# Dequantization of units 11 to 41 by chains of Prelu, with GpSimd taking the first right pass and the high half, and the kernel's maximum through TensorE

## What is computed

```python
xn = _layernorm(x)                       # x: (4, 512, 512) f32, 2048 tokens of 512
K  = _s4_kernel(...)                     # 512 numbers from 64 complex states
y  = irfft(rfft(xn, 1024) * rfft(K, 1024))[..., :512] + D * xn     # causal convolution
Wg, Wu = dequant_nf4(gate), dequant_nf4(up)     # (1792, 512) each, 4-bit codes as int32
Wd     = dequant_nf4(down)                      # (512, 1792), one absmax for 64 codes
h  = silu(xn @ Wg.T) * (xn @ Wu.T)
out = x + y + h @ Wd.T
```

## Time and profile before

| what | value |
|---|---|
| median of 3 runs | 467.42 us (466.54 to 467.91) |
| the profiled execution | 466.52 us, of which the profile's span is 464.7 us |
| PE busy | 446.5 us, 96% of the span |
| DVE busy | 400.2 us, 86% |
| ACT busy | 284.9 us, 61% |
| GpSimd busy | 61.5 us, 13% |
| TensorE clock granted | 1.0 in every stretch |

### The profile page before, as it was taken

How to read it: one execution, slowest core, us unless ns; L and a number is a source line. 1 busy time by engine, 2 the same in 40 slices (tenths; PEclk the granted TensorE clock), 3 DMA queues, 4 the chain that set the end, 5 groups by cost and what they waited for, 6 DMA issues and landing times.

```text
span 464.7 us, 7186 instructions
## 1 busy us (share of the span) xinstructions
PE 446.5 (96%) x2595; PEld 253.9 (55%) x2595; DVE 400.2 (86%) x658; ACT 284.9 (61%) x480; POOL 61.5 (13%) x116
## 2 busy tenths in 40 slices
PE   0699999999999999999999999999999999999997
PEld 0554444444444444444444444466544688888886
DVE  4899689979798887988999888876799899999993
ACT  7966565587597965769777696794132543545340
POOL 0464499400000000000001000023100000000000
PEclk9999999999999999999999999999999999999999
DMA  8482545122425234112132225256570021101111
GB/s 273 86 284 80 114 88 147 47 70 67 159 69 181 95 132 158 59 56 86 51 95 71 91 41 158 78 183 209 169 292 0 1 92 47 44 3 47 47 47 45
DMA packets 31830, 47.20 MB, mean 102 GB/s; under 512 B 13044, under 2 KB 14132, under 8 KB 31284
## 3 DMA queue, kind: packets, MB, share of 16 engines
q1 hardware_dynamic: 30516, 42.56, 30.0%
q0 software_dynamic: 1280, 4.20, 2.8%
HBM read 35.93 MB, written 8.72 MB: 96 GB/s over the span
## 4 chain that ended last, share of the span: by engine, by line
PE 90%; DVE 3%; POOL 2%; ACT 2%; DMA 1%; issue 1%; SPq 0%; POOLq 0%
PE bank L1875 34%; PE bank L2006 21%; PE bank L2108 21%; PE bank L2059 8%; PE bank L2049 6%; DMA work<-in_q_up 1%; POOL h L718 1%; PE bank L1910 1%; ACT h L816 0%; DVE h L1174 0%; DVE h L1337 0%; PE bank L1965 0%; DVE bank L1281 0%; DVE work L1167 0%; DVE work L1163 0%
## 5 line engine op out<-in xcount | busy, mean ns | idle before, releaser
L1875 PE MATMUL bank<-xT,w 128*128 128x512 f16 (+1 forms) x732 | 164.9, 378 | 1.9 <-DVE w L1174 1.7
L1875 PEld LDWEIGHTS bank<-xT,w 128*128 128x128 f16 x732 | 71.9, 99 | 86.5 <-DVE w L1174 2.1
L816 ACT ACTIVATE work<-work 128x512 f32<-128x512 int32 x136 | 77.8, 623 | 5.0 <-DVE work L1146 2.5
L2108 PE MATMUL bank<-wd,work 128*128 128x256 f16 x504 | 56.2, 273 | 0.0
L2108 PEld LDWEIGHTS bank<-wd,work 128*128 128x128 f16 (+1 forms) x504 | 49.3, 98 | 6.0
L2006 PE MATMUL bank<-h 128*128 128x512 f16 x198 | 48.1, 379 | 0.0
L1106 ACT ACTIVATE work<-h 128x896 f16<-128x896 f32 x30 | 27.9, 942 | 27.8 <-DVE h L1783 18.3
L2108 PE MATMUL bank<-h,work 128*128 128x256 f16 x378 | 42.2, 273 | 0.0
L2108 PEld LDWEIGHTS bank<-h,work 128*128 128x128 f16 x378 | 37.0, 98 | 4.3
L900 ACT ACTIVATE work<-bank,sc 128x512 f32<-128x512 f32 x45 | 30.4, 678 | 13.2 <-PE bank L1875 12.9
L2059 PE MATMUL bank<-wd,h 128*128 128x512 f16 x168 | 36.4, 379 | 0.0
(11 more groups left out here) (183 smaller groups left out, 643.3 us busy)
## 6 DMA issues: line engine op xcount, KB each, us to landing
h<-in_x SPq DMA_DIRECT2D x8, 512.0 KB, 6.2
moved<-h SPq DMA_DIRECT2D x4, 1024.0 KB, 4.7
xT<-in_x POOLq DMA_DIRECT2D x16, 256.0 KB, 3.4
h<-moved SPq DMA_DIRECT2D x4, 1024.0 KB, 10.5
out<-xT SPq DMA_DIRECT2D x15, 256.0 KB, 2.1
work<-in_q_gate SPq DMA_DIRECT2D x14, 256.0 KB, 2.7
work<-in_q_up SPq DMA_DIRECT2D x14, 256.0 KB, 2.9
work<-in_am_gate SPq DMA_DIRECT2D x28, 128.0 KB, 3.0
```

The lines of the kernel that those rows point to most:

```text
L816: nc.scalar.activation(knee_of(u, k), qs[:, u % 2, :], KNEE, scale=scale, bias=bias, alpha=below).then_inc(knee_done, 1)
L1875: mm = nc.tensor.matmul(out_b, weights(k)[:, unit, wl, f, :], xT[:, TPC * c + first:TPC * c + last, xl, f, :], start=(i == 0), stop=(i == ...
L2108: mm = nc.tensor.matmul(out_b, part, w, start=(n == 0), stop=(n == 3 * KT - 1))
```

## The change

- **CHAINED** becomes `range(11, UNITS)`: the units 11 to 41 are made by chains, not only the last four. Rooms for the whole tile rotate over three (`whole_of`).
- **The right chain** loses its first Prelu on ACT. GpSimd makes it as `max(code, c) - c` from the codes (`first_pass`, `L818` of the changed kernel), and ACT goes on from its result: six passes in the order l0 r0 l1 r1 l2 r2, where r0 waits for `first_done`.
- **The high half** of the units 11 to 37 (POOL_HALVES) moves from ACT to GpSimd (`weight_hi` there, `L831`); DVE's low half waits for `phi_done`. DVE's items of such a unit u are now WHOLE(u), low half of u-1, SCALED(u).
- **GpSimd's list** in the windows is first pass of u+1, then high half of u, for u = 11..37. `turned_rows()` (the eight copies) is called inside this loop, after the high half of unit 28. First passes of units 39 and 40 stand ahead of the reloads of x, that of 41 behind the fourth.
- **The maximum** over partitions: PE transposes the column of row maxima (`kernel_max`) after product 1 of window 13, DVE reduces and makes the powers in slot 2, PE spreads two numbers to all partitions by a matmul with ones (`kernel_scale`) after product 6, DVE makes the scales in slot 4 and the Toeplitz tiles in slot 5 of window 13 (before: slot 1). `ones` gets a room of its own.

```diff
-CHAIN_ORDER = ("r0", "l0", "r1", "l1", "r2", "l2", "r3")
+CHAIN_ORDER = ("l0", "r0", "l1", "r1", "l2", "r2")
-CHAINED = range(UNITS - 4, UNITS)
+CHAINED = range(11, UNITS)
+POOL_HALVES = range(CHAINED[0], UNITS - 4)
...
+        def room_read(u):
+            return dq_after(u - 1, LEFT) if u == CHAINED[0] else dq_after(u - 2, WHOLE)
...
-                if u >= 2:
-                    sp.wait_ge(knee_done, PASSES_AT[u - 2] + (2 if u - 2 in CHAINED else KNEES))
+                if u - 2 in CHAINED:
+                    sp.wait_ge(first_done, u - 2 - CHAINED[0] + 1)
+                    sp.wait_ge(knee_done, PASSES_AT[u - 2] + 1)
...
-            pool.wait_ge(u_done, 4)
-            for c in range(2):
-                for a in range(4):
-                    ...
-            pool.wait_ge(t_done, 3)
-            pool.partition_all_reduce(kmax, krow, P, bass.bass_isa.ReduceOp.max).then_inc(kmax_done, 1)
+            def first_pass(u):
+                pool.wait_ge(q_ld[u % 2], 16 * (u // 2 + 1))
+                pool.wait_ge(dq_done, room_read(u))
+                pool.tensor_scalar(chain_room(u, "r"), qs[:, u % 2, :], RIGHT_FROM, RIGHT_FROM,
+                                   ALU.max, ALU.subtract).then_inc(first_done, 1)
+            def weight_hi(u):
+                pool.wait_ge(dq_done, dq_after(u, SCALED))
+                ...
+                pool.tensor_scalar(weight_of(u)[HI], whole_of(u), scale_of(u), None, ALU.mult).then_inc(phi_done, 1)
+            pool.wait_ge(v_done, V_STEPS)
+            first_pass(CHAINED[0])
+            for u in POOL_HALVES:
+                first_pass(u + 1)
+                weight_hi(u)
+                if u == made_before(NM - 3) - 1:
+                    turned_rows()
+            first_pass(UNITS - 3)
+            first_pass(UNITS - 2)
             for t in range(NT):
                 pool.wait_ge(conv_done, t + 1)
                 pool.dma_start(res[:, t, :], x_v[:, t, :]).then_inc(xr_ld[t], 16)
+                if t == 3:
+                    first_pass(UNITS - 1)
...
+                elif side == "r":
+                    act.wait_ge(first_done, u - CHAINED[0] + 1)
...
                     if u in CHAINED:
-                        i += 2
+                        i = (3, 2, 4)[i]
...
+                if k == NM - 1:
+                    kernel_max()
...
+                if k == NM - 1:
+                    kernel_scale()
```

More of the change, by code:

```diff
@@ L133 @@
 DVE_AT = counted(lambda u: 3 if u in CHAINED else 5)
+ACT_HALVES = [u for u in range(UNITS) if u not in POOL_HALVES]
 ACT_AT = counted(lambda u: 1 + (u not in CHAINED) + (PASSES_AT[u + 2] - PASSES_AT[u + 1] if u + 1 < UNITS else 0))
@@ L214, in ffn_conv_kernel @@
         sc = sb("sc", [P, 34], F32)
+        ones = sb("ones", [3, P], F32)
         V = sb("V", [P, 2, 8], F32)
@@ L663, in _ @@
         def _(pool):
-            pool.memset(one3, 1.0).then_inc(one_done, 1)
+            pool.memset(ones[:], 1.0).then_inc(one_done, 1)
             pool.memset(ident[:], 0.0).then_inc(one_done, 1)
@@ L785, in _, with turned_rows @@
                 chained(pool.tensor_copy(V_halves[rows, :, 8 * half:8 * half + 8], V[rows]))
-            pool.wait_ge(u_done, 4)
-            for c in range(2):
-                for a in range(4):
-                    if a == 0:
-                        row = turns[:, 0, c:c + 1].to_broadcast([P, 4])
-                    else:
-                        row = turns[:, a, c:c + 3 * a + 1:a]
-                    pool.tensor_copy(turned[:, c, a, :], row).then_inc(turn_done, 1)
-            pool.wait_ge(t_done, 3)
-            pool.partition_all_reduce(kmax, krow, P, bass.bass_isa.ReduceOp.max).then_inc(kmax_done, 1)
+            def turned_rows():
+                pool.wait_ge(u_done, 4)
+                for c in range(2):
+                    for a in range(4):
+                        if a == 0:
+                            row = turns[:, 0, c:c + 1].to_broadcast([P, 4])
+                        else:
+                            row = turns[:, a, c:c + 3 * a + 1:a]
+                        pool.tensor_copy(turned[:, c, a, :], row).then_inc(turn_done, 1)
+            def first_pass(u):
[5 more added lines that the diff above has]
+                pool.wait_ge(dq_done, dq_after(u, SCALED))
+                unit = SEQ[u]
+                if unit < GU:
+                    before = room_before(unit // 2)
+                    if unit % 2 and before in BLOCKED:
+                        pool.wait_ge(m_done, m_at(before, 4))
+                    else:
+                        pool.wait_ge((gate_done, up_done)[unit % 2], WHOLE_COUNT[LAST_USE[before]])
+                pool.tensor_scalar(weight_of(u)[HI], whole_of(u), scale_of(u), None, ALU.mult).then_inc(phi_done, 1)
[8 more added lines that the diff above has]
+            first_pass(UNITS - 2)
             for t in range(NT):
@@ L805, in _ @@
             act.wait_ge(one_done, 1)
-            nc.scalar.activation(sil[0:1, 0, 0:1], one3[0:1, 0:1], ACT.Silu)
+            nc.scalar.activation(sil[0:1, 0, 0:1], ones[0:1, 0:1], ACT.Silu)
             def make_knee(u, k):
@@ L857, in weight_hi, with gate_copy @@
                 nc.scalar.activation(weight_of(u)[HI], whole_of(u), ACT.Copy, scale=scale_of(u)).then_inc(whi_done, 1)
-                if unit < GU and unit % 2 == 0 and unit // 2 in BLOCKED:
-                    k = unit // 2
-                    if k == BLOCKED[0]:
-                        act.wait_ge(xlo_done, NT)
-                    else:
-                        act.wait_ge(xs_lo, 4)
-                        act.wait_ge(w_done, 4 * blocked(k))
-                    nc.scalar.activation(sums_room(k)[0], whole_of(u), ACT.Copy, scale=scale_of(u)).then_inc(g_done, 1)
+            def gate_copy(u):
+                if SEQ[u] >= GU or SEQ[u] % 2 or SEQ[u] // 2 not in BLOCKED:
+                    return
+                k = SEQ[u] // 2
+                act.wait_ge(dq_done, dq_after(u, SCALED))
+                if k == BLOCKED[0]:
+                    act.wait_ge(xlo_done, NT)
+                else:
+                    act.wait_ge(xs_lo, 4)
+                    act.wait_ge(w_done, 4 * blocked(k))
+                nc.scalar.activation(sums_room(k)[0], whole_of(u), ACT.Copy, scale=scale_of(u)).then_inc(g_done, 1)
             def items(first, last):
@@ L874, in items @@
                     if p == ACT_AT[u]:
[L875 removed]
+                        if u - 1 in ACT_HALVES:
+                            weight_hi(u - 1)
+                        gate_copy(u - 1)
                     elif i == 0:
@@ L1916, in _ @@
             pe.wait_ge(sc_done, 7)
-            nc.tensor.matmul(bank[0][:, P:P + 6], one3, dg3, start=True, stop=True).then_inc(mx_bc, 1)
+            nc.tensor.matmul(bank[0][:, P:P + 6], ones[:], dg3, start=True, stop=True).then_inc(mx_bc, 1)
             turn(2)
@@ L1967, in kernel_line, with kernel_max, kernel_scale @@
                 mm.then_inc(toe_mm, 1)
+            def kernel_max():
+                pe.wait_ge(t_done, 3)
+                nc.tensor.transpose(bank[7][0:1, 0:P], krow, ident[:]).then_inc(km_tp, 1)
+            def kernel_scale():
+                pe.wait_ge(sc_done, KMAX_MADE)
+                nc.tensor.matmul(bank[7][:, P:P + 2], ones[0:1, :], sc[0:1, 17:19], start=True, stop=True).then_inc(km_bc, 1)
             def blocked_product(k, i):
```

63 lines of the change are left out of this document (40 added, 23 removed).

## The result

The changed kernel takes 473.11 us (median of 4, 472.24 to 473.30) against 467.09 us for the kernel before: 1.0124 times as long, interval 1.0103 to 1.0144, so 6.0 us more. The profiled execution took 473.30 us with a span of 471.5 us. I had forecast 470.0 us within 467.6 to 472.6: the direction was right, the size not, and the result lies outside the range.

The account below looks back on a forecast made before the run. PE was taken as the bound, busy 96% of the span and without a gap from 48 us on. Window 11's 1.8, window 4's 0.4 and the maximum's 0.4 made 2.6 us on 467.42: 470.0 us, range 467.6 to 472.6.

Parts of the forecast that it names:

- It can shorten the time only in the first 48 us, which it leaves alone but for one memset: Whole kernel: from 48 us PE has no gap, so the change is worth at most nothing.
- My third rival: Start: PE's wait for the identity shrinks with the reduction gone, 1.5 us at most, 466.3 us; chance 0.04.
- Window 11, 1.8 us: Ahead of product 3: unit 30's first pass queues behind the eight copies, the join comes late, PE waits 1.8 us.
- Window 4, 0.4 us: Window 3 into 4: r0 of unit 11 delays chunk 3's silu and the last `block_lo`; PE loses 0.4 us.
- Slow passes: Rival, windows 11 and 4 and fifth reload: GpSimd passes at 2.2 us add 2.5 us, 472.5 us; chance 0.14.
- Steady windows at nothing: Steady windows: GpSimd keeps up; PE would wait in every window only if a pass took over 3.4 us.
- The maximum: Window 13: two instructions added to PE's gapless row, 0.45 us if neither waits, taken as 0.4.
- The convolution: First passes of units 39 to 41 delay reloads of x, mostly hidden: 0, at most 0.7 us.
- DVE's busy time: Sign over the whole kernel: DVE's busy time lower by about 32 us, about 27 units x 2 x 0.6.
- the median I used: Starting point of the forecast for the kernel before: 467.42 us, to which 2.6 us were added.

Follow-up runs that it names:

- the old maximum: Changed kernel with GpSimd's reduction for the maximum again, ahead of unit 33's high half, copies behind unit 30's first pass, chunk 3's silu ahead in window 3: 479.37 us.
- the forms: Changed kernel with seven forms of a 128x512 step on GpSimd, three times each, behind the last reload of x, results not needed: 477.19 us.

## Why the prediction was wrong

- **"It can shorten the time only in the first 48 us, which it leaves alone but for one memset"**: this step failed, and with it the forecast. The reduction stands at 283 us in the kernel before, but its removal also takes away a stop of 9 us at 1.2 us, and without it GpSimd's chain of small steps beside DVE took 9.5 us and not 7.65, in every kernel that was run. It cost 2.9 us in the profiled execution: 1.3 us of late tokens and 1.6 us of lower clock; with the reduction put back the kernel took 470.63 us. My third rival had seen the tie between the reduction and the wait for the identity, and drew the wrong sign from it: the identity came at 1.3 us, PE then waited for DVE (10.0 us), and nothing was gained.
- **Window 11, 1.8 us**: measured 1.9 as a wait and 2.0 as PE's delay, by the mechanism named, and the run that moves the copies shows it. Two terms were off and nearly cancel, which is luck: the copies took 1.04 us and not 2.07, and the pass 2.31 and not 0.76 to 1.46. Before, DVE had step behind step beside the copies; now it was idle for the first 0.3 us and then ran one step on a bank. That this is why they were short is not shown. The quarter turn's end (forecast 249.3; it came at 253.65, which less the shift of 4.2 us that this window had by then is 249.4) and the way from the pass to the join's end (5.0 us for 5.1 to 5.2) were right. ACT's idle time ahead of r0 was 4.1 us for some 3.
- **Window 4, 0.4 us**: right place and chain of causes, mis-sized: 1.2 as a wait and 1.3 as PE's delay. The pass took 1.94 us, and DVE's steps beside the pass of unit 12 lost 0.35 us (L1267 0.83 for 0.48). With 1.94 us for 0.76 to 1.46 in the sum of the prediction the silu is 1.3 us late, and 1.3 + 0.35 - 0.46 = 1.2; 0.14 us from the block's end to PE's start, which the sum left out, make it 1.3. The rival of slow passes had given 1.1.
- **Slow passes**, 0.14: their size came true (2.08 us on the mean), their effect in window 11 did not add up, because of the copies. I had put too little on it: no row showed this form, and of the rows of 0.76 to 1.43 us I took both ends for bounds.
- **Steady windows at nothing**: right; no wait of PE but the two, with passes under the 3.4 us named. **The maximum**: 0.5 for 0.45 us. **The convolution**: right; no wait, although the first reload went out at 317.7 us, 1.5 later than forecast once the shift of 6.25 us is taken off. **DVE's busy time** fell by 26.2 us for the 32 named.
- Without the start the loss would have been 3.8 us (1.3 + 2.0 + 0.5) for my 2.6, which makes 471.3 us from the median I used, inside the range. My range had no room for a part of the kernel that I had declared untouched.

## What to carry to other kernels

Removing an instruction can change stretches far away from it, here one 270 us ahead of it: look at both ends of that engine's list, and at the kernel's start, before calling a stretch untouched. A chain of small GpSimd steps beside a full DVE list is not a sum of durations but a row of boundaries hit or missed; one memset of 0.1 us ahead of it made it 1.9 us longer here, and a chain on which PE waits does not belong there. Relief for an engine that is not the bound (26 us of DVE) gave nothing; what counted were two places where a wait had been put ahead of a step that PE needs, and both could be mended by order alone.

## What the runs showed of the hardware

- A GpSimd reduction over partitions came with a stop elsewhere: 9.15 to 10.16 us ahead of the affine_select at the start where it was the last thing that GpSimd computed (four kernels), and 7.0 us behind it, with none at the start, where other computing steps followed (one kernel). Without a reduction there was no stop.
- A 128x4 step on GpSimd takes 0.2 us alone and up to 1.41 beside DVE's 128x512 steps, and ends 0.15 us behind the start of one of them.
- A second idle stretch of PE of about 1 us at 28 us can go with a fall of the granted clock to 1.2 GHz right behind it. Of the executions of kernels with the long chain (the old maximum and the forms left out) 32 of 63 had the mean clock of 0.996, and five traces with it show the fall between 29 and 34 us; of those with the short chain (the kernel before among them) none of 73. It cost 1.6 us. A mean of 0.992 or 0.993 came with either chain, in 5 of 63 and 11 of 73; the one trace of it shows the fall earlier, at 20 to 27 us, behind idle stretches of PE of 2.1 and 1.0 us.
- A 128x512 max/subtract on GpSimd takes 1.9 us or more from int32 and float32 alike, multiply/add 0.9 to 1.3 beside a busy DVE.
